# Decoder layer: exponentials transposed and multiplied with v before the projection

## The reference

```python
h = (x - mu) / jnp.sqrt(var + LN_EPS) * norm_w + norm_b
qkv = h @ qkv_w.T + qkv_b
q, k, v = (qkv[..., 0, :], qkv[..., 1, :], qkv[..., 2, :])
w = jax.nn.softmax(jnp.einsum('ncq,nck->nqk', q, k * scale), axis=2)
a = jnp.einsum('nqk,nck->ncq', w, v)
return a @ proj_w.T + proj_b + x
```

## Time and profile before

| | us |
|---|---|
| median of 3 runs | 772.17 |
| lowest and highest | 769.93, 772.34 |
| profiled execution, its own time | 772.46 |
| its span, from first to last instruction | 770.7 |

### The profile page before, as it was taken

One profiled execution on the slowest core, in us unless ns is written; L12 is line 12 of the kernel. 1 busy time (PEld: TensorE's weight loads), 2 busy tenths in 40 slices (PEclk: granted clock), 3 DMA queues, 4 the chain that ended last, 5 costly groups with the idle time before them and its releaser, 6 DMA issues. The chain is left out here.

```text
span 770.7 us, 13351 instructions
## 1 busy us (share of the span) xinstructions
PE 697.5 (91%) x4496; PEld 616.0 (80%) x4496; DVE 499.2 (65%) x1264; ACT 394.9 (51%) x891; POOL 384.1 (50%) x554
## 2 busy tenths in 40 slices
PE   3779989989989899899899885799999999999997
PEld 2669879978878788788788774678888888888886
DVE  5675765865865856757668665667666766667442
ACT  4855746756666658457566524424333343334321
POOL 2676866685677667657757510322232323232222
PEclk9989999999999999999999996999999999999999
DMA  7622322313212303213100128222130312221200
GB/s 214 180 81 82 103 65 65 112 31 93 91 48 80 104 24 115 69 55 110 43 22 1 51 66 268 75 110 82 63 112 21 136 54 112 80 110 55 111 28 28
DMA packets 50768, 64.47 MB, mean 84 GB/s; under 512 B 3800, under 2 KB 49416, under 8 KB 49840
## 3 DMA queue, kind: packets, MB, share of 16 engines
q1 hardware_dynamic: 50736, 64.06, 26.1%
HBM read 56.60 MB, written 7.45 MB: 83 GB/s over the span
## 5 line engine op out<-in xcount | busy, mean ns | idle before, releaser
L1427 POOL TENSOR_TENSOR sg<-sg,cw_wide 128x512 f32<-128x512 f32 x56 | 74.0, 1321 | 187.5 <-ACT sg L1384 177.7
L1388 ACT ACTIVATE a_hi<-af 128x512 fp32r<-128x512 f32 x63 | 39.8, 632 | 156.8 <-DVE af L1508 156.8
L76 PE MATMUL bank<-h_hi,w_lo 128*128 128x512 f32 x224 | 92.1, 411 | 7.1 <-DVE w_lo L1525 5.2
L810 POOL TENSOR_TENSOR ctxt_lo<-ctxtf,ctxt_hi 128x375 fp32r<-128x375 f32 x64 | 58.7, 939 | 64.5 <-ACT ctx_hi L607 56.2
L77 PE MATMUL bank<-h_lo,w_hi 128*128 128x512 f32 x224 | 89.6, 400 | 0.0
L78 PE MATMUL bank<-h_hi,w_hi 128*128 128x512 f32 x224 | 89.3, 399 | 0.0
L1508 DVE TENSOR_TENSOR af<-bank,sg 128x512 f32<-128x512 f32 x63 | 43.2, 686 | 62.2 <-POOL sg L1427 59.1
L1513 DVE TENSOR_TENSOR a_lo<-af,a_hi 128x512 fp32r<-128x512 f32 x63 | 48.1, 763 | 34.9 <-ACT a_hi L1388 34.9
L815 POOL TENSOR_TENSOR ctx_lo<-ctxf,ctx_hi 125x256 fp32r<-125x256 f32 x96 | 69.9, 756 | 0.0
L76 PE MATMUL bank<-w_hi,a_lo 128*128 128x256 f32 x224 | 63.2, 282 | 0.0
L77 PE MATMUL bank<-w_lo,a_hi 128*128 128x256 f32 x224 | 63.2, 282 | 0.0
(11 more groups left out here) (254 smaller groups left out, 2316.5 us busy)
## 6 DMA issues: line engine op xcount, KB each, us to landing
cw_wide<-cw_scratch SPq DMA_DIRECT2D x7, 2048.0 KB, 7.2
ctxtf<-in_ctx_t SPq DMA_DIRECT2D x32, 375.0 KB
ctxf<-in_ctx SPq DMA_DIRECT2D x32, 375.0 KB
xt<-in_x SPq DMA_DIRECT2D x8, 448.0 KB, 3.7
x_scratch<-x2b SPq DMA_DIRECT2D x8, 448.0 KB, 3.3
x2n<-x_scratch SPq DMA_DIRECT2D x7, 512.0 KB, 4.6
x2t<-x_scratch SPq DMA_DIRECT2D x7, 512.0 KB, 3.9
out_dram<-x2t SPq DMA_DIRECT2D x7, 512.0 KB, 2.9
```

The source lines that it names most:

```text
L76: pe.matmul(dst, a_lo, b_hi, start=first, stop=False, **kw)
L810: last_lo = pool.tensor_tensor(ctxt_lo[:, j, k, 0:S], ctxtf[:, j, k, :], f32(ctxt_hi[:, j, k, 0:S]), ALU.subtract)
L1388: act.activation(a_hi[n % (AHEAD + 1)][:, :], af[(p + n) % 2][:, :], ACT.Copy).then_inc(a_hi_ok, 1)
L1427: pool.tensor_tensor(sg[b][:, :], sg[b][:, :], cw_wide[p][:, ORDER[n], :], ALU.mult).then_inc(sgw_ok, 1)
```

## The change

The three matrices are multiplied from the other side. The exponentials are no longer written over the scores but into SBUF, into the tile `h3`, whose rows of the layer norm are used up by then (`ew`, two buffers, taken in turn by the streams). PE transposes them (`turn_w`, four transposes of 128 by 128 in a stream) back into the stream's bank; ACT and DVE split the transposed exponentials without the reciprocals (`exp_high`, `exp_low`, one instruction each over 512 columns where there were two of 256). `values` multiplies them with v: the stationary operand has 128 columns and the moving one is v of one stream, 112 columns, in 12 matmuls. The reciprocals now come in when that product is split (`values_high`, `values_low`, two instructions of 112 columns each), and `attention_out` is the product with the projection: 6 matmuls with 112 stationary and 256 moving columns. Besides, from group 1 on, the two v products stand among the q/k products instead of behind the scores. The parts that waited for v and for `wp_lo` change places too.

```diff
@@ names
+            ew = [h3[:, KB * b:KB * (b + 1), :] for b in range(2)]
@@ PE, products of one stream
-                    def probs_proj(j):
+                    def turn_w(j):
+                        pe.wait_ge(exp_ok, ev[j])
+                        for m in range(KB):
+                            for half in range(KB):
+                                n = m * D + half * P
+                                last = pe.transpose(bank[j][:, n:n + P], ew[j % 2][:, half, m * P:(m + 1) * P], ident[:, :])
+                        last.then_inc(t_w, 1)
+
+                    def values(j):
+                        if j == 0:
+                            pe.wait_ge(v_lo_ok, KB * (i + 1))
+                        pe.wait_ge(w_lo_ok, ev[j])
+                        t = slice(j * L, (j + 1) * L)
+                        for half in range(KB):
+                            for m in range(KB):
+                                n = slice(m * D + half * P, m * D + (half + 1) * P)
+                                last = mm3(pe, bank[j][:, half * L:(half + 1) * L], op_hi[j][:, n], op_lo[j][:, n],
+                                           v_hi[:, m, t], v_lo[:, m, t], m == 0, m == KB - 1)
+                        last.then_inc(av_mm, 1)
+
+                    def attention_out(j):
...
-                        pe.wait_ge(w_lo_ok, ev[j])
+                        pe.wait_ge(av_lo_ok, ev[j])
                         for half in range(KB):
-                            for q in range(KB):
-                                n = slice(q * D + half * P, q * D + (half + 1) * P)
-                                last = mm3(pe, bank[j][:, half * D:(half + 1) * D], op_hi[j][:, n], op_lo[j][:, n],
-                                           wp_hi[:, q, :], wp_lo[:, q, :], q == 0, q == KB - 1)
-                        last.then_inc(g_mm, 1)
-
-                    def attention_out(j):
...
-                        for k in range(KB):
-                            n = slice(k * D, (k + 1) * D)
-                            last = mm3(pe, bank[j][0:L, 0:D], v_hi[:, k, t], v_lo[:, k, t], op_hi[j][:, n], op_lo[j][:, n],
-                                       k == 0, k == KB - 1)
+                            n = slice(half * L, (half + 1) * L)
+                            last = mm3(pe, bank[j][0:L, 0:D], op_hi[j][:, n], op_lo[j][:, n], wp_hi[:, half, :], wp_lo[:, half, :],
+                                       half == 0, half == KB - 1)
                         last.then_inc(ao_mm, 1)
@@ PE, order of a group
                     qk_product(1)
+                    if not is_first(i):
+                        v_product(0)
                     qk_product(2)
+                    if not is_first(i):
+                        v_product(1)
                     qk_product(3)
...
                     scores(3)
-                    v_product(0)
+                    if is_first(i):
+                        v_product(0)
+                        v_product(1)
+                    else:
+                        z_q2c(i - 1, 0)
+                    turn_w(0)
                     if not is_first(i):
-                        z_q2c(i - 1, 0)
                         z_q2c(i - 1, 1)
-                    probs_proj(0)
-                    v_product(1)
-                    probs_proj(1)
-                    probs_proj(2)
+                    turn_w(1)
+                    values(0)
+                    turn_w(2)
+                    values(1)
                     attention_out(0)
-                    probs_proj(3)
+                    turn_w(3)
+                    values(2)
                     attention_out(1)
+                    values(3)
                     attention_out(2)
@@ ACT
-                            e = act.activation(bank[j][:, n], bank[j][:, n], ACT.Exp, bias=smx[:, j, half:half + 1],
+                            e = act.activation(ew[j % 2][:, half, :], bank[j][:, n], ACT.Exp, bias=smx[:, j, half:half + 1],
...
-                    def probs_high(j):
-                        act.wait_ge(sinv_ok, ev[j])
-                        for half in range(KB):
-                            n = slice(half * D, (half + 1) * D)
-                            w = act.activation(op_hi[j][:, n], bank[j][:, n], ACT.Copy, scale=sinv[:, j, half:half + 1])
-                        w.then_inc(w_hi_ok, 1)
+                    def exp_high(j):
+                        act.wait_ge(t_w, ev[j])
+                        act.activation(op_hi[j][:, :], bank[j][:, :], ACT.Copy).then_inc(w_hi_ok, 1)
...
-                    def probs_proj_high(j):
-                        act.wait_ge(g_mm, ev[j])
-                        act.activation(op_hi[j][:, :], bank[j][:, :], ACT.Copy).then_inc(g_hi_ok, 1)
+                    def values_high(j):
+                        act.wait_ge(av_mm, ev[j])
+                        act.wait_ge(sinv_ok, ev[j])
+                        for half in range(KB):
+                            n = slice(half * L, (half + 1) * L)
+                            w = act.activation(op_hi[j][:, n], bank[j][:, n], ACT.Copy, scale=sinv[:, j, half:half + 1])
+                        w.then_inc(av_hi_ok, 1)
@@ DVE
+                    def exp_low(j):
...
+                        dve.tensor_tensor(op_lo[j][:, :], bank[j][:, :], f32(op_hi[j][:, :]), ALU.subtract).then_inc(w_lo_ok, 1)
+
+                    def values_low(j):
+                        dve.wait_ge(av_hi_ok, ev[j])
                         for half in range(KB):
-                            n = slice(half * D, (half + 1) * D)
+                            n = slice(half * L, (half + 1) * L)
                             w = dve.scalar_tensor_tensor(op_lo[j][:, n], bank[j][:, n], sinv[:, j, half:half + 1], f32(op_hi[j][:, n]),
                                                          ALU.mult, ALU.subtract)
-                        w.then_inc(w_lo_ok, 1)
+                        w.then_inc(av_lo_ok, 1)
```

More of the change, by code:

```diff
@@ L682, in group @@
                     else:
+                        v_high(0)
                         x4_high(i - 1)
                     qk_high(2)
+                    if not is_first(i):
+                        v_high(1)
                     qk_high(3)
@@ L1018, in group @@
                         ln1_stats(i + 1, 1)
+                    if not is_first(i):
+                        v_low(0)
                     qk_low(2)
@@ L1021, in group @@
                         ln1_stats(i + 1, 2)
+                    if not is_first(i):
+                        v_low(1)
                     qk_low(3)
@@ L1060, in group @@
                     x1_moments(0)
-                    probs_proj_low(3)
+                    if is_first(i):
+                        wl_low(2)
+                    values_low(2)
+                    if not last and not is_first(i):
+                        ln1_moments(i + 1)
                     x1_sum(1)
```

61 lines of the change are left out of this document (25 added, 36 removed).

## The result

The changed kernel took **779.3 us** (median of 5 runs, 777.75 to 781.27) against 772.34 for the kernel before (median of 5): a ratio of 1.0092, with a 95% interval from 1.0072 to 1.0112. It is slower by 7.0 us. The forecast was 777.4, within 771 to 804.

A forecast was written before the change was run, and what follows sets the result against it. The prediction took PE's own work plus a few waits as the bound. Groups 1 to 7 at +0.7 us each (+4.9), group 0 about 0 and rounding +0.3 gave +5.2 on 772.17, 777.4 us, range 771 to 804.

The forecast's parts named there:

- The price of the short product: 48 `values` products a group with 112 moving columns: 0.110 us each, set by the stationary load, 5.28 us a group.
- Rival 1: Short fp32r products in `values` run at the f32 rate, 0.187 us each: total +30, 802 us; chance 0.23.
- rival 2: `values` products faster, their load hidden or quick: 768.6 us at 0.052 us each, +0.8 us at 0.091; chance 0.09.
- the quick load: Stationary load for `values` at 0.091 us, the quickest in the rows: +0.8 us in all, no change; half of 0.09.
- The transposes: 16 added PE transposes of 128 by 128 a group, 0.110 us each, 1.76 us.
- PE's work and waits in an inner group: Work -5.71 + 1.76 + 5.28 = +1.3 us, waits 0.65 less: +0.7 us a group in groups 1 to 7.
- the wait for v: PE's wait in the attention, 0.47 + 0.09 us a group, falls away with v products among the q/k products.
- Rival 3: PE's clock falls once in each of seven groups, some 1.7 us each: +12, 789 us; chance 0.07.
- the announced sign: For the forecast: granted PE clock 1.00 in groups 2 to 6.
- Group 0: The 2.7 us wait for `wp_lo` goes, two of 1.2 us arise for split values: -0.1 us, counted as nothing.
- The layout: Lists of all engines laid out with measured durations to predict waits; -0.1 us in group 0, rounding +0.3 in all.
- The sum: Groups 1 to 7 +4.9 us, group 0 about 0, rounding +0.3: +5.2 us in all, experts untouched.

The follow-up runs named there:

- values_64: The changed kernel with only the first 64 of each 128 stationary columns in the products of `values`, half the result's rows left out; 769.37 us.
- turn_w_twice: The changed kernel with every transpose of the exponentials in `turn_w` made twice, 16 more a group; 788.2 us.
- v_behind: The changed kernel with both v products back behind the scores in every group; 779.43 us.
- values_256: The changed kernel with 256 instead of 112 moving columns in every product of `values`; 779.48 us.
- wl_late: The changed kernel with the splits of the last product's weights moved out of the attention of group 0; 778.34 us.
- before_v_early: The kernel before with only the v products moved among the q/k products, from group 1 on; 781.57 us.
- before_c_order: The kernel before with lists reordered only from `turn_c(0)`, `c_high(0)` and `x1_sum(0)` on, the attention half as before; 769.61 us.
- before_reordered: The kernel before with the same products but another order of the lists of PE, ACT and DVE from group 1 on; 762.31 us.

## Why the prediction was right, and where it was not

**The price of the short product** was the open term, and the value taken held: 0.110 forecast, 0.111 measured. values_64 bears out the reason given, that the load sets it. Rival 1 (0.187) and both forms of rival 2 (0.052, and 0.091 for the quick load) are out by that distance. One number of rival 2 is off by its own account: between its two points, -3.6 us at 0.052 and +0.8 at 0.091, a gain of 2.3 us comes under 0.064, not about 0.07.

**The transposes** were 0.110 forecast and 0.11 measured. In turn_w_twice 16 more of them cost 1.1 us a group, the 1.76 of work less what fell into waits.

**PE's work and waits in an inner group.** Forecast +1.3 and -0.65, together +0.7; measured 54.22 - 53.45 = +0.77, or 7 x 0.77 = 5.4 where the sum had 4.9. PE's busy time rose by 50.52 - 49.34 = 1.18 and its time without work fell by 0.39, from 4.11 to 3.72; the slow restarts behind the waits count as busy in these two, so they split the same change in another way than the sum did. The waits ahead of `values(0)` (0.4) and `values(2)` (0.25), and none ahead of `turn_c(0)`, came as announced. ACT and DVE have less to do, as the prediction says, but not by much: 34.00 us in a group instead of 34.29, and 35.37 instead of 36.15.

**A reason that was wrong without harm.** The prediction says that the wait for v "falls away with the v products among the q/k products". It falls away in v_behind as well, where both v products are back behind the scores. There `values(0)` stands behind two z products and eight transposes, and v's splits ahead of those of the exponentials; which of the two is needed was not tested.

**The clock was a term that the sum left out.** Rival 3 had one fall in each of seven groups at 1.7 us, chance 0.07, and the announced sign for the forecast was a clock of 1.00 in groups 2 to 6. Two inner groups had a fall, and each cost 0.8 us, 1.6 in all: the sign did not come true, the mechanism happened in part, and its price was half, since the wait for POOL behind it went. The step that didn't hold is "The new attention gives PE less to stream ... Against: in 120.4 to 124.0 ... the clock stayed 1.00": I asked whether the transposes would let the clock fall, and turn_w_twice gives no sign that they do. But the falls come elsewhere, behind the waits for `cw_lo`, in work that both kernels have, and the kernel before has one there too. The mean clock of the changed kernel's five runs is 0.972 to 0.979, their median 0.975; that of the kernel before is 0.977 to 0.986 in the three sets, with medians of 0.980 to 0.982. So over the runs it does spend more time at half clock. Why is not shown: the change may only shift when the waits come. values_256 does not show that the columns matter, since wl_late has no fall in groups 1 to 6 with the same products as the changed kernel.

**Group 0** was counted at nothing and took 2.1 us more. The kernel before had there

```profile
19.12:79.24 60.12, 49.94 (x330) 44.90 (x331) 39.38 (x105) 37.87 (x93) 41.95 (x66) 0.94 0.41 115
```

against 53.29 us busy in 62.25 for the changed one. The layout did give the new waits, at 1.2 us each: PE waited 2.7 us there for `values_low` and 1.9 for `exp_low`, and no more for `wp_lo`, and PE's time without work fell from 10.18 to 8.96 us. The busy time rose by 3.35 us, where the work that was added is 1.3. The rest is time at half clock, 13.6 us (10.2 and 3.4) where the kernel before had 6.8. Whether the clock is the cause stays open: before_v_early, before_c_order and before_reordered, whose group 0 is that of the kernel before, had 10.2 us at half clock in it and took 59.8 to 59.9 us, no more than 60.1; there the slower PE only filled its waits. wl_late has both less waiting and less half clock and doesn't part them.

**The sum.** Group 0 +2.1, groups 1 to 6 +6.2 (of which 1.6 is the clock), group 7 +0.3, where this time the kernel before had the fall, and the experts -1.3: +7.4 in the span. The experts' code is the same, but the -1.3 is hardly scatter: they took 313.6 to 315.2 us in the profiles of the seven kernels with the new products and 315.2 to 316.9 in the six with the old ones. Between the kernel before and the changed one 1.2 of it has arisen by the 200th matmul, 57 to 58 us into the experts, where PE's longest waits of that part lie (for `h`, `h_lo` and `w_lo`); why is not shown. The forecast of +5.2 was right in sign and in its main term. That it came within 1.9 us of the median is luck in part: group 0 and the experts, both counted at nothing, offset each other by more than half, and of the two falls in the changed kernel the one in the kernel before takes back half.

## What to carry to other kernels

A product with few moving columns still pays for a full load of its stationary operand (0.111 us with 112 moving columns, 0.118 with 256, and 0.059 with half of the stationary ones): count loads first, then columns. A product that is independent of the chain is worth its place as cover: the same move cost 10 us in one kernel and nothing in the other, and two partial reorderings gave 2 us each where both together gave 10. When the waits hang on chains of several engines, lay out all lists at once with measured durations before rewriting the mathematics; here the order was worth more than the change.

## What was unexpected of the hardware

The same stretch of work, 1.88 us of PE in 3.40, was followed by half clock in one group and by full clock in the next. So of identical groups some are 0.8 us longer, and which ones differs between kernels that do much the same work (the third and sixth steps of the changed kernel; the second, fourth and sixth in v_behind; none of the inner ones in values_256 and wl_late, the latter with the same lists from group 1 on as the changed kernel). The mean clock of the changed kernel's runs goes with their times: 781.27 us at 0.972, 777.75 at 0.979. And 256 moving columns cost hardly more than 112 for the same load, 0.118 against 0.111 us.
